# Third norm of a decoder layer: from VectorE to ScalarE as scale and bias, with two small bias products on GpSimd

## The reference

```
x = _layernorm(x + _L0_attn_ref(x, Wq, Wk, Wv, Wo))        # norm 1
x = _layernorm(x + _L0_xattn_ref(x, ctx_512, ctx_512))     # norm 2
x = _layernorm(x + _L0_ffn_ref(x, ln_w, ln_b, W1, b1, W2, b2))   # norm 4, around the block below

def _L0_ffn_ref(inputs, ln_w, ln_b, W1, b1, W2, b2):
    x = bf16_round(inputs)
    h = mx_layernorm(x, ln_w, ln_b)     # norm 3: (x - mu) * rsqrt(var + eps) * w + b, rounded to bf16
    h = mx_linear(h, W1, b1)            # both operands quantised in blocks of 32
    h = mx_gelu(h)
    h = mx_linear(h, W2, b2)
    return bf16_round(residual + h)
```

## Time and profile before

| | us |
|---|---|
| median of 3 runs | 291.15 (291.07 to 294.93) |
| the profiled execution, its own time | 292.19 |
| its span | 290.40 |
| PE busy in the span | 271.7 |
| DVE busy | 256.2 |
| ACT busy | 226.4 |
| POOL busy | 174.6 |

### The profile page before, as it was taken

How to read it: one execution, slowest core, us unless ns; L and a number is a source line. 1 busy time by engine, 2 the same in 40 slices (tenths; PEclk the granted TensorE clock), 3 DMA queues, 4 the chain that set the end, 5 groups by cost and what they waited for, 6 DMA issues and landing times.

```text
span 290.4 us, 5342 instructions
## 1 busy us (share of the span) xinstructions
PE 271.7 (94%) x1640; PEld 165.5 (57%) x1640; DVE 256.2 (88%) x678; ACT 226.4 (78%) x386; POOL 174.6 (60%) x253
## 2 busy tenths in 40 slices
PE   7899998999998999999989998999699989997799
PEld 3776755476565775667556756575346444543354
DVE  3489899996999799999999999989996998799982
ACT  5551768479997699988998899889998899875650
POOL 2737291687466687868786878667777353533321
PEclk9999999999997999999999999999959999999999
DMA  7930200002110020022002200210010000100111
GB/s 238 393 113 2 99 3 0 10 5 71 37 43 0 0 79 15 2 65 77 11 5 64 79 9 5 67 43 9 7 36 5 2 1 0 37 2 1 38 37 38
DMA packets 11053, 12.68 MB, mean 44 GB/s; under 512 B 3216, under 2 KB 8336, under 8 KB 10768
## 3 DMA queue, kind: packets, MB, share of 16 engines
q1 hardware_dynamic: 10592, 11.55, 12.5%
q10 hardware_dynamic: 432, 0.79, 0.7%
HBM read 9.84 MB, written 2.10 MB: 41 GB/s over the span
## 4 chain that ended last, share of the span: by engine, by line
PE 55%; DVE 25%; ACT 7%; issue 6%; POOL 3%; DMA 3%; DVEq 0%; POOLq 0%; ACTq 0%
PE bank L2141 8%; PE bank L2175 8%; PE bank L2188 5%; DVE nm L1343 5%; PE bank L2075 4%; PE bank L2026 3%; PE bank L2062 3%; PE bank L2254 3%; PE bank L2101 3%; DVE st L1298 3%; PE bank L2229 2%; PE bank L2088 2%; PE bank L2125 2%; PE bank L2196 2%; DMA xT<-mT 2%
## 5 line engine op out<-in xcount | busy, mean ns | idle before, releaser
L1343 DVE TENSOR_REDUCE nm<-bank 128x4 f32<-128x512 f32 x128 | 84.0, 678 | 3.0 <-PE bank L2141 2.6
L878 ACT ACTIVATE p_sb<-bank 128x512 f32<-128x512 f32 x128 | 72.2, 600 | 11.1 <-PE bank L2175 10.5
L2141 PE MATMUL bank<-kbd,xT 96*128 96x512 f32 x128 | 56.2, 470 | 2.2 <-ACT xT L849 1.5
L2175 PE MATMUL bank<-xT,kbd 104*128 104x512 f32 x128 | 53.4, 448 | 4.6 <-DMA xT<-mT 3.1
L557 POOL TENSOR_TENSOR kbd<-k3r,diag_sb 96x512 fp32r<-96x512 f32 x32 | 33.5, 1061 | 11.4 <-PE bank L2175 11.4
L2175 PEld LDWEIGHTS bank<-xT,kbd 104*128 104x128 f32 x128 | 24.7, 194 | 18.1 <-ACT p_sb L878 5.9
L2141 PEld LDWEIGHTS bank<-kbd,xT 96*128 96x128 f32 x128 | 24.6, 195 | 16.4 <-DVE nm L1343 9.3
L2188 PE MATMUL bank<-p_sb,va_sb 128*32 128x512 f32 x256 | 33.7, 616 | 0.0
L511 POOL TENSOR_TENSOR rs<-ve,nhalf 128x2 f32<-128x2 f32 (+1 forms) x36 | 26.1, 724 | 4.6
L506 POOL TENSOR_SCALAR ve<-mv 128x2 f32<-128x2 f32 (+1 forms) x36 | 8.4, 233 | 33.4 <-DVE mv L1304 31.7
L2062 PE MATMUL bank<-wkv_r,xt_r 128*128 128x512 f32 x84 | 23.7, 404 | 0.0
(11 more groups left out here) (135 smaller groups left out, 619.6 us busy)
## 6 DMA issues: line engine op xcount, KB each, us to landing
xt_sb<-in_xt SPq DMA_DIRECT2D x8, 256.0 KB, 2.9
x_sb<-in_x SPq DMA_DIRECT2D x8, 256.0 KB, 2.9
out_dram<-o_sb SPq DMA_DIRECT2D x7, 256.0 KB, 2.2
k_sb<-in_ctx SPq DMA_DIRECT2D x8, 192.0 KB, 2.9
x_all<-in_w SPq DMA_DIRECT2D x1, 1024.0 KB, 5.2
w_raw<-in_w SPq DMA_DIRECT2D x1, 1024.0 KB, 7.3
p_sb<-in_wkv ACTq DMA_DIRECT2D x2, 256.0 KB, 4.1
cv_sb<-in_ctxv SPq DMA_DIRECT2D x8, 64.0 KB, 2.0
```

What stands on the lines that cost most here:

```text
L878: sc.activation(p_sb[:, k, :], bankB[k % 2][:, :], ACT.Exp, scale=SCORE_SCALE).then_inc(s_ex, 1)
L1343: ve.tensor_reduce(nm[:, b, u, g, :], bankA[(2 + k + 11 * b) % 2][:, :].rearrange("p (k t) -> p k t", k=KU), AX.X, ALU.max, negate=True).t ...
L2141: mm(bankA[(2 + k + 11 * b) % 2][:, :], xT[0:MR, b, u, g, :], kbd[0:MR, b, u, :, :].rearrange("r k t -> r (k t)"), start=True, stop=True). ...
L2175: mm(bankB[k % 2][:, :], kbd[0:MR + 2 * KU, b, u, kk, :], xT[0:MR + 2 * KU, b, u, :, :].rearrange("r g s -> r (g s)"), start=True, stop=Tr ...
```

## The change

For pairs 0 to 6, `norm3` leaves DVE's list. POOL computes a bias for each row right after `rstd` (`shift_product` and `shift` into a new tile `nb3`), and ACT applies scale and bias in a new `pair_norm3`, once for each batch. `weight3` waits for both as before. Pair 7 keeps its norm on DVE.

```
+            def pair_norm3(p, b):
+                act.wait_ge(s_nb3, 2 * p + 2)
+                sc.activation(h0_sb[:, b, :], batch_of(xb_all, p, b), ACT.Identity, bias=nb3[:, 1, b:b + 1],
+                              scale=rs3[:, b:b + 1]).then_inc(s_h0, 1)
 # POOL, in head (pair 0), step (p[4]) and tail (pairs 5 and 6)
                 rstd(p[4], ve3, rs3, s_ve3, s_rs3)
+                shift_product(p[4], mv3, rs3, nb3, s_rs3, s_nb3)
+                shift(p[4], nb3, s_nb3)
                 weight3(p[4])
 # ACT, head
                 exps(1, 0, 6)
+                pair_norm3(0, 0)
+                pair_norm3(0, 1)
                 exps(1, 0, 7)
 # ACT, step
                     exps(p[3], 0, 6)
+                if on[4]:
+                    pair_norm3(p[4], 0)
+                    pair_norm3(p[4], 1)
+                if on[3]:
                     exps(p[3], 0, 7)
 # ACT, tail, pair 5
                 exps(6, 0, 7)
+                pair_norm3(5, 0)
+                pair_norm3(5, 1)
                 maxT(6, 1)
 # ACT, tail, pair 6
+                pair_norm3(6, 0)
                 exps(7, 1, 0)
+                pair_norm3(6, 1)
                 exps(7, 1, 1)
 # DVE: head after max_high(1, 1) and max_low(1, 1); step after quantise_g(p[5], 1, 9);
 # tail after max_low(6, 1) and after quantise_g(5, 1, 9)
-                norm3(p, 0)
-                norm3(p, 1)
```

More of the change, by code:

```diff
@@ L104, in decoder_kernel @@
         nb2 = sb("nb2", [P, 2, PB], F32)
+        nb3 = sb("nb3", [P, 2, PB], F32)
         nb4 = sb("nb4", [P, 2, PB], F32)
@@ L274, in decoder_kernel @@
         s_nb2 = sem("shift2")
+        s_nb3 = sem("shift3")
         s_nb4 = sem("shift4")
@@ L662, in head @@
                 rstd(0, ve3, rs3, s_ve3, s_rs3)
+                shift_product(0, mv3, rs3, nb3, s_rs3, s_nb3)
+                shift(0, nb3, s_nb3)
                 weight3(0)
@@ L738, in tail @@
                 rstd(5, ve3, rs3, s_ve3, s_rs3)
+                shift_product(5, mv3, rs3, nb3, s_rs3, s_nb3)
+                shift(5, nb3, s_nb3)
                 weight3(5)
@@ L757, in tail @@
                 rstd(6, ve3, rs3, s_ve3, s_rs3)
+                shift_product(6, mv3, rs3, nb3, s_rs3, s_nb3)
+                shift(6, nb3, s_nb3)
                 weight3(6)
@@ L1622, in head @@
                 max_high(1, 1)
-                norm3(0, 0)
                 max_low(1, 1)
-                norm3(0, 1)
                 quantise_weight(1, 0, 2)
@@ L1703, in step @@
                     quantise_g(p[5], 1, 9)
-                if on[4]:
-                    norm3(p[4], 0)
-                    norm3(p[4], 1)
                 if on[3]:
@@ L1826, in tail @@
                 max_low(6, 1)
-                norm3(5, 0)
-                norm3(5, 1)
                 quantise_h(5, 0)
@@ L1893, in tail @@
                 quantise_g(5, 1, 9)
-                norm3(6, 0)
-                norm3(6, 1)
                 denominators(7, 0)
```

## The result

The changed kernel takes 297.93 us in the median of 4 runs (297.74 to 298.23), beside 291.11 us for the kernel before on the same chip (291.07 to 294.93). The ratio is 1.0203, with a 95% interval from 1.0158 to 1.0248: it is slower, and whether by more or less than 2% the runs don't tell. The forecast was 295.6 with a range of 290.5 to 298.2: the sign and the kind of mechanism were right, the size was 2.3 us too small.

What follows compares the result with a forecast made beforehand. It took a ring through DVE and POOL from quantise_h to quantise_h as the bound, PE nearly as tight. Terms 0.7 - 0.2 + 2.4 + 0.9 + 0.7 = 4.5 us gave 296.7 profiled, 295.6 median; range 290.5 to 298.2.

Steps and rivals of the forecast that it cites:

- Nothing comes back from DVE: The 4.55 us leaving DVE's list over seven pairs count as zero, becoming a longer wait of quantise_h for shift3.
- the first rival: DVE's list decides: weight3 starts earlier and the whole 4.55 us come back, giving 286.6 us; chance 0.10.
- A step costs 0.8: In steps 2 to 4 weight3 and quantise_h start 0.8 us later through POOL and ACT, 2.4 us in all.
- the upper bound of 0.84: Highest price of a step, in us, if DVE's quantising product holds up POOL's bias product; the lower bound was 0.51.
- It costs nothing on top there: ACT's later exponential 7 moves PE's weigh by 0.3 to 0.6 us, under the 0.5 to 0.84 of the ring.
- the ring: Loop closing each step: quantise_h, DVE's list to the statistics, POOL's reciprocal deviation, norm, weight3, shift3, next quantise_h; 0.8 us longer.
- Step 1, -0.2: In step 1 weight3 starts earlier by the new way, a gain of 0.2 us, bounds 0 and 0.5.
- Pair 0 and pair 5, 0.7 and 0.9: Losses in us from later weight3 at these pairs; bounds 0.3 to 1.1 and 0.5 to 1.1.
- Pair 6, 0.7: weight3 starts 1.4 us later, DVE has slack behind it, so a loss of 0.7; bounds 0.3 and 1.4.
- the second rival: ACT's gaps and DVE instructions no longer stretched beside POOL's take up the delay; 290.5 to 293 us; chance 0.22.
- The third rival: ACT's list decides: the full delay behind the norms reaches PE, 6.8 us together, 297.9 on the median; chance 0.20.
- both signs: Signs of the third rival: PE's weigh waits for exponentials, and DVE idles at places other than quantise_h.

Runs made afterwards that it cites:

- e5: The changed kernel with DVE's quantising product of g one maximum earlier in the steps, ahead of maxima 5; 298.79 us, ratio 1.0230 to the kernel before.
- e12: The changed kernel with DVE's quantising product of g behind maximum 6 in the steps; 298.87 us, ratio 1.0255 to the kernel before.
- the reference: Profile of the kernel before with two unused POOL bias instructions more for each pair, full clock in every step; 291.39 us, ratio 1.0006.
- e9: The kernel before plus POOL's bias and 14 spare ACT activations that wait for it; weight3 doesn't wait for them; 296.21 us, ratio 1.0142.
- e1: The kernel before plus 14 spare ACT activations at the places of the change, without a wait for a bias; 293.0 us, ratio 1.0059.
- e6: The changed kernel with pair 5's norm back on DVE, without its bias and ACT norms; 296.16 us, ratio 1.0155 to the kernel before.
- e4: The changed kernel with exponential 7 ahead of the two norms on ACT in the steps; 304.69 us, ratio 1.0468 to the kernel before.
- e10: The kernel before with norm3 one maximum later on DVE in the steps, behind maxima 6; 294.76 us, ratio 1.0094.
- e11: The kernel before with norm3 ahead of DVE's quantising product of g in the steps; 294.46 us, ratio 1.0102.

## Why the prediction was right in kind and too small

**Nothing comes back from DVE: right.** DVE's 4.2 us turned into waiting; steps of 30.4 us exclude the first rival. (For that rival the text asks for more than 1.5 us between the reciprocal deviation and norm3; its own terms, 1.88 less 0.73 and 0.14, make 1.0. In steps 2 to 4 there were 0.5, so nothing hangs on it.)

**A step costs 0.8: right.** It is 0.87 in steps 2 to 4 (2.62 in three). The way through POOL and ACT is 2.27 us from the end of the reciprocal deviation to weight3, against 1.38: 0.89 more, 0.05 above the upper bound of 0.84. The bound's reason held as well: the product was held by DVE's neighbour (0.56, against 0.20 in e5, where DVE runs maxima beside it). By the lock that the Trainium skill describes on the page SBUF — State Buffer, in Who interferes with whom, a VectorE instruction with two inputs in SBUF blocks a GpSimd one that reads there; the rows of e5 and e12 agree, 1.23 for 0.69 and back.

**"It costs nothing on top there", of ACT's list: the step of the argument that failed, without cost in steps 2 to 4.** I took the delay of exponential 7 as 0.9 to 1.2 and the gaps behind it as cover. In the reference exponential 7 starts 0.80 behind the end of the reciprocal deviation (124.73 to 125.53), in the changed kernel 2.03 behind it (126.38 to 128.41), 1.2 more, and the cover is 0.5 of that: e9, in which it is the only delay, has steps 0.7 to 0.8 longer. As this ends beside the ring's 0.8, the sum hardly noticed it. It is why the wait of quantise_h came out at 10 and not 16 us: 7.0 of it stand at q_times_sum. e1 and e9 differ in one wait: not ACT's 1.0 us of work is dear, but standing in order at a bias that comes 1.0 us after the reciprocal deviation.

**Step 1, -0.2: wrong for the median, measured +0.84.** I read the earlier trace rows as a place where the new way is shorter, because weight3 started 2.47 behind the reciprocal deviation there. That belongs to executions in which the clock falls at this place: TensorE's granted clock was 0.89 in two windows of it, so for a part of them it ran at the lower of its two levels, 1.2 and not 2.4 GHz. The rows give start:end, length, busy PE, PEld, DVE, ACT and POOL, clock, DMA; first of the kernel before, then of the reference.

```profile
85.00:92.00 7.00, 5.55 (x29) 4.28 (x28) 6.91 (x23) 6.65 (x13) 4.54 (x11) 0.89 0.07 25
92.00:100.00 8.00, 8.00 (x56) 4.96 (x55) 6.94 (x17) 4.60 (x7) 4.34 (x6) 0.89 0.00 0
```
```profile
85.00:92.00 7.00, 5.55 (x32) 3.87 (x30) 7.00 (x23) 6.62 (x13) 4.54 (x11) 1.00 0.06 20
92.00:100.00 8.00, 7.98 (x64) 5.17 (x64) 7.34 (x18) 5.72 (x10) 6.18 (x9) 1.00 0.00 0
```

In the kernel before the granted clock is 1.00 up to 90 us and lower from 90 to 94. PE was idle for most of the two us ahead of that in both executions (busy for 0.54 and 0.66), so I see nothing that the engine did otherwise before the clock fell. DVE waited for PE's scores, norm3 behind it was late, and the step took 29.45 us instead of 28.36. At full clock weight3 starts 1.38 behind the reciprocal deviation in step 1 as in steps 2 to 4:

```profile
94.41 0.69 POOL L513 TENSOR_TENSOR rs<-ve,nhalf 128x2 f32<-128x2 f32 x1
...
96.48 1.28 POOL L597 TENSOR_TENSOR h_sb<-h_sb,lnwb_sb 128x512 f32<-128x512 f32 x1 [0.39 <-DVE h_sb L1391]
```

What I took for a property of step 1 was in the page, as one 7 among the nines of the clock's line at this place. It is no rare event: e1 and e6 have the same fall (0.83 from 90 to 100 us). In e1, which has the norm on DVE, weight3 again starts 2.53 behind the reciprocal deviation and step 1 takes 29.87. In e6, whose step 1 is the changed kernel's, it starts 1.90 behind, where I had reckoned 1.88, and step 1 takes 29.18, no more than at full clock (29.20; step 2 takes 0.3 more). So where the clock falls the term about holds, from 29.45 to 29.18; what failed was to carry it over to the median of 291, which belongs to executions at the higher mean clock. It also explains why the profiled time, forecast at 296.7 and measured at 297.80, missed by less than the median: the execution I started from was 1.1 us longer than the median.

**Pair 0 and pair 5, 0.7 and 0.9: right,** with 0.64 and 0.89.

**Pair 6, 0.7: mis-sized, 2.11 with the recovery at the end.** Two terms. 1.42 lie between the statistics of pair 6 and its quantise_h (5.36 in the reference, 6.78 in the changed kernel), the 1.4 worked out from the earlier trace rows; I halved it for slack behind it. Of that slack, 0.3 was real (the last stretch), as the instruction of 1.08 in the reference takes 0.73 in the changed kernel. The other 0.98 arises ahead of pair 6, as a consequence of pair 5: the product of h beside ffn_out; with pair 5 undone, 0.87 of it goes (e6). I had looked for stretched instructions that would relax (the second rival), not for ones that would be held where they had not been.

**The third rival** gave 297.9 and the median is 297.93, but it isn't confirmed by that. It put 1.2 on each of steps 2 to 4 (measured 0.87), nothing on step 1 (0.84) and 1.0 on pair 6 (2.11); its errors cancel. Its mechanism is real and ties with the ring, and both signs that it named are there: PE's weigh waits 0.64 for exponential 7, and DVE idles at q_times_sum. What remains open is the price of the pairs 0 and 6 alone, which only the trace gives.

## What to carry to other kernels

Before counting moved work as free because the receiving engine has idle time, ask what it has to wait for in its order: the same two instructions cost nothing in a step as spare work (1.9 us in the whole kernel, outside the steps 2 to 4) and 0.7 to 0.8 in each step with a wait for a late input in front (4.2 in the whole). Where a kernel is balanced, follow the delay down every list of the waiting engine to the common end, and look one stage further for pairs of VectorE and GpSimd instructions that it pushes on to each other. Read the clock of each stretch before taking a row from it, and repeat an odd stage in a second execution: one low digit made what is a loss at full clock look like a gain.

## What the runs showed of the hardware

VectorE and GpSimd held each other up where both had operands in SBUF, and in all the rows below it was the instruction that started later, by 0.01 to 0.5 us in the trace, that got longer.

GpSimd first: a VectorE instruction then ended 0.03 to 0.28 us behind GpSimd's. 0.17 became 1.17 (128x16) and 0.29 became 1.13 (128x512) in e4, a cast of 128x32 went from 0.24 to 1.03 in e12 and from 0.30 to 0.88 in e10, 0.30 became 1.22 (128x32) in e11, and 0.43 became 1.41 (the product of h, 128x512) in the changed kernel. VectorE first: a GpSimd product of 128x2 went from 0.20 to 0.56 (changed kernel) and a reciprocal deviation from 0.69 to 1.23 (e5) beside a VectorE product of 0.68, and ffn_out from 1.15 to 1.36 (reference).

Not every pair is held. Two maxima, which read PSUM, take 1.28 beside the bias of the changed kernel as in the kernel before, and the first instruction of quantise_h, which reads 128x512 from SBUF, takes 0.69 beside POOL's keys (131.38) and 0.69 with POOL idle (254.47).

Where several lines end close together, as in this kernel, such a collision of up to 1 us is as large as the 0.9 that the change costs in a step. Of the reorderings tried here, e5 and e12 removed one and brought another; e6 removed the one of pair 5 by taking that pair's change back.
